# Cross-attention kernel: the products with the value table move ahead of the output pieces in every step

## What is computed

```python
q = heads(x @ W_q);  k_t = heads(text @ W_k);  v_t = heads(text @ W_v)
probs_t  = softmax(einsum('bhsd,bhtd->bhst', q, k_t) * scale)
text_out = einsum('bhst,bhtd->bhsd', probs_t, v_t)
k_ip = heads(ip @ W_k_ip);  v_ip = heads(ip @ W_v_ip)
qsem = l2norm(einsum('bhst,bte->bhse', probs_t, text))
sem  = einsum('bhse,bne->bhsn', qsem, l2norm(ip))
probs_ip = softmax(q_dot_k_ip * scale + 0.5 * sem) * mask
out = (text_out + probs_ip @ v_ip) @ W_out + b_out + x
```

## Time and profile before

| | us |
|---|---|
| median of 3 runs | 1018.13 (1018.01 to 1019.59) |
| the profiled execution | 1019.44 |
| its span | 1017.4 |
| TensorE busy (matmul, weight load) | 967.3, 800.9 |
| VectorE, ScalarE, GpSimd busy | 822.7, 695.2, 659.7 |
| wait of TensorE's U for `pts` | 12.6 in 20 waits |
| wait of VectorE for U | 99.8 in 106 waits |

### The profile page before, as it was taken

The page is one execution under the profiler, slowest core; times in us unless marked ns, Lnnn a source line. Parts: engine busy times, 40 slices in busy tenths (PEclk is TensorE's granted clock), DMA queues, the critical chain, the costliest instruction groups (busy, mean ns, idle before and its releaser), DMA issues.

```text
span 1017.4 us, 24927 instructions
## 1 busy us (share of the span) xinstructions
PE 967.3 (95%) x7684; PEld 800.9 (79%) x7684; DVE 822.7 (81%) x2409; ACT 695.2 (68%) x2332; POOL 659.7 (65%) x1906
## 2 busy tenths in 40 slices
PE   6986888999999999999999999999999999999988
PEld 6865676888888888888878888888878888888855
DVE  5895788888888887888888888878878888888763
ACT  4545787777777777777767777777776777767730
POOL 3342577766766677677766767676766667667761
PEclk9999999999999999999999999999999999999989
DMA  8946999988799989979899989898899988887863
GB/s 283 314 164 140 189 171 197 173 174 173 156 193 192 189 171 184 171 165 176 173 187 175 193 171 177 169 178 170 177 172 191 187 171 188 142 161 137 158 123 111
DMA packets 488147, 180.27 MB, mean 177 GB/s; under 512 B 449694, under 2 KB 467155, under 8 KB 488015
## 3 DMA queue, kind: packets, MB, share of 16 engines
q1 hardware_dynamic: 487983, 178.63, 86.6%
q10 hardware_dynamic: 32, 0.07, 0.0%
HBM read 42.34 MB, written 27.22 MB: 68 GB/s over the span
## 4 chain that ended last, share of the span: by engine, by line
PE 77%; DMA 5%; ACT 3%; DVE 3%; SPq 2%; issue 2%; POOL 0%; DVEq 0%; ACTq 0%
PE ps_Q L1364 25%; PE ps_O L1253 25%; PE ps_S L1274 12%; PE ps_U L1350 11%; DMA pts<-ph 3%; PE ps_M L1290 3%; ACT pr L1034 2%; DMA x_in<-in_x_dram 1%; ACT ph L1046 1%; SPq L947 1%; SPq L910 1%; DVE bias L1156 0%; PE ps_U L1253 0%; SPq L966 0%; DVE x_in L1141 0%
## 5 line engine op out<-in xcount | busy, mean ns | idle before, releaser
L1034 ACT ACTIVATE pr<-ps_S,bias 128x73 f32<-128x73 f32 x1280 | 288.9, 340 | 103.4 <-DVE bias L1156 102.1
L1116 POOL TENSOR_TENSOR ph<-pr,ph 128x220 f16<-128x220 f32 (+1 forms) x640 | 274.1, 460 | 125.8 <-ACT ph L1046 125.8
L1364 PE MATMUL ps_Q<-xT,wq_hi 128*128 128x512 f32 x800 | 279.2, 414 | 6.3 <-DVE qT L1123 6.3
L1253 PE MATMUL ps_O<-wo_hi,aT 128*128 128x320 f16 x1220 | 281.1, 301 | 0.0
L1046 ACT ACTIVATE ph<-pr 128x292 f16<-128x292 f32 x640 | 241.4, 501 | 0.0
L1253 PE MATMUL ps_O<-wo_lo,aT 128*128 128x320 f16 x610 | 183.5, 301 | 0.0
L1364 PEld LDWEIGHTS ps_Q<-xT,wq_hi 128*128 128x128 f32 x800 | 145.6, 190 | 33.4 <-DVE qT L1123 7.6
L1350 PE MATMUL ps_U<-xm,pts 128*128 128x110 f16 (+1 forms) x2560 | 158.8, 212 | 13.3 <-DMA pts<-ph 12.6
L1350 PEld LDWEIGHTS ps_U<-xm,pts 128*128 128x128 f16 (+1 forms) x2560 | 144.4, 98 | 30.5 <-issue 9.2
L1274 PEld LDWEIGHTS ps_S<-kbd,qT 128*128 128x128 f32 x960 | 151.3, 189 | 18.8 <-issue 3.0
L1274 PE MATMUL ps_S<-kbd,qT 128*128 128x308 f32 x960 | 163.7, 305 | 2.6 <-ACT pr L1034 2.1
(11 more groups left out here) (228 smaller groups left out, 1343.2 us busy)
## 6 DMA issues: line engine op xcount, KB each, us to landing
out_dram<-x_in SPq DMA_DIRECT2D x64, 320.0 KB, 2.6
x_in<-in_x_dram SPq DMA_DIRECT2D x56, 320.0 KB, 3.2
pts<-ph SPq DMA_TRANSPOSE x320, 3.4
w_k<-in_L_xattn_W_k_dram SPq DMA_DIRECT2D x5, 512.0 KB, 9.4
w_ip<-in_L_xattn_W_k_ip_dram SPq DMA_DIRECT2D x1, 2560.0 KB, 11.2
w_v<-in_L_xattn_W_v_dram SPq DMA_DIRECT2D x5, 512.0 KB, 8.7
w_ip<-in_L_xattn_W_v_ip_dram SPq DMA_DIRECT2D x1, 2560.0 KB, 10.5
x_in<-in_x_dram SPq DMA_DIRECT2D x2, 1280.0 KB, 5.8
```

Source lines behind the costliest of these rows:

```text
L1034: last = nc.scalar.activation(pr[p % P_RING][:, j, h, :], sc[:, j, h, 0:T], ACT.Exp, bias=bias[p % 2][:, j, h:h + 1], scale=SCALE)
L1116: nc.gpsimd.tensor_tensor(lo, full[:, :, t0:t1], one[:, :, 0, t0:t1], ALU.subtract).then_inc(pl_ready, 1)
L1253: last = nc.tensor.matmul(bank[:, 0:HALF], stationary, moving, start=(k, a, b_) == O_MMS[0], stop=(k, a, b_) == O_MMS[-1])
L1364: last = nc.tensor.matmul(ps_Q[:], wq[a][:, c, k * P:(k + 1) * P], xT[(CC * i + c) % XT_RING][b_][:], start=(c, a, b_) == Q_MMS[0], stop=( ...
```

## The change

In TensorE's loop the block U, with its waits, moves from behind O (and the end pieces) to ahead of O, behind S and M. So the order within a step was S, M, O, U, Q and is S, M, U, O, Q. Nothing else is changed: the same matmuls, semaphores, buffers and the loops of the other engines.

```diff
                     last.then_inc(xT_ready, 1)
 
+                u = pair_of(p - LU)
+                if u is not None:
+
+                    slot = u // 2
+                    k0 = slot % CC
+                    if u % 2 == 0 and slot % SLOTS < CC:
+                        pe.wait_ge(xm_loaded[k0], 32 * (slot // SLOTS + 1))
+                    if u:
+                        pe.wait_ge(attn_ready, u)
+                    else:
+                        pe.wait_ge(xT_lo, CC)
+                    for j in range(2):
+                        pe.wait_ge(*ring(pts_loaded[j], u))
+                        for h in range(HG):
+                            for tile, n in enumerate(STACK):
+                                last = nc.tensor.matmul(uo[:, j, h, :], pts[u % PT_RING][0:n, j, 2 * h + tile, :],
+                                                        xm[0:n, tile, k0 * HG + h, :], start=tile == 0, stop=tile == 1)
+                    last.then_inc(u_ready, 1)
+
                 for i, half, piece in out_at(p):
...
                     if part == 3:
                         last.then_inc(o_ready, 1)
 
-                u = pair_of(p - LU)
-                if u is not None:
...
-                    last.then_inc(u_ready, 1)
-
                 if q_at(p) is not None:
```

## The result

The changed kernel took 1020.17 us in the median (1017.07 to 1025.37), against 1017.98 us (1014.47 to 1021.32) of the kernel before, measured beside it: a ratio of 1.0026 [1.0015, 1.0038]. It is slower by 0.26%, 2.2 us by the medians. Forecast were 1018.9 us and "within 0.2%"; the time lies in the range, 1.3 us above the forecast, and just outside the band of no change. Two kernels further down each had one execution far longer than all its others (1929.69 and 1595.92 us), which their medians leave out.

The account below looks back on a forecast made before the run. The matmul engine's own blocks, one behind the other, were taken as the bound. Terms -8.5 + 1.3 + 6.0 + 2.5 - 0.5 = +0.8 us, applied to the 1018.13 median, gave 1018.9 us; range 1012.0 to 1025.5, the forecast's own 1016 to 1021.

Parts of the forecast that it names:

- joint U to Q becomes O to Q: Steps 16 to 157: O's last matmul covers Q's f32 weight load, saving 0.06 us a step, -8.5 us.
- joint S to U: New joint where U follows the scores: costed at nothing, bound one U matmul, 0.05 us a step.
- waits for VectorE: Middle of the run: the matmul engine doesn't wait for VectorE, so nothing was charged.
- step 16: First step with O: U(14) loses its cover of 12 O matmuls and waits for pts, +1.3 us once.
- three changes of batch: Steps 34-42, 74-82, 114-122: SyncE's queue paces landings, O no longer covers the wait, +2.0 us each, +6.0.
- single late transposes: Nine of 160 pairs, pair 52 standing for them, have pts landing 0.1 to 1.0 us late: +2.5 us.
- end: After S(159): the 2.4 us aT wait goes, about 2 lost as U(158) waits for pts, -0.5 us.
- The sign that I named for it: Profile after, query block: second query matmul comes 0.235 us after the first, not 0.31.
- the upper end: Batch changes at 2.8 us each instead of 2.0: 17 matmuls of cover lost, and half clock after the wait.
- The joints win: Rival: earlier VectorE moves even pairs' landings ahead, late transposes vanish, batch changes cost 1.2 each; 1013.2 us, chance 0.31.
- U waits in every turn: Rival: pts landings late in every turn of ten steps, 0.6 us in each of 14 tiles; 1027.2 us, chance 0.19.
- No joint is gained: Rival: O followed by Q leaves the weight load as open as U did, 0 for -8.5; 1027.4 us, chance 0.12.

Follow-up runs that it names:

- one-matmul order: U placed behind all output matmuls of the step but the last, against the kernel before: 1010.45 us, ratio 0.9922.
- without the loads: Batches 1 to 3 without kbd and xm loads, on batch 0's tables: kernel before 1008.74 us, changed kernel 1004.32, U ahead of the last output matmul 999.43.

## Why the prediction came out as it did, point by point

| term | forecast, us | the runs show |
| --- | --- | --- |
| joint U to Q becomes O to Q | -8.5 | -9.3 (one-matmul order, both without loads) |
| joint S to U | 0 | 0 (0.010 in half of the steps, as S to O had before) |
| waits for VectorE | none | +2.3 (0.12 a turn, and 0.6 in step 151) |
| step 16 | +1.3 | +1.2 (shift of the trace from step 16 to 17) |
| three changes of batch | +6.0 | +6.6 (2.2 each) |
| single late transposes | +2.5 | 1.6 (the view of the waits) to 3.0 (U's distance from S or M) |
| end | -0.5 | +0.3, within 1.3 of nothing |
| sum | +0.8 | +2.2 measured; the rows above give +2.7 to +4.1 |

**The joints.** The mechanism is right. The size, 0.066 us a step instead of 0.06, was within its ends: 0.061 of it is the surplus behind U, worked out below. The sign that I named for it, the distance from the first query matmul to the second, was wrong. I wrote that the second query matmul would come 0.235 us after the first; it comes after 0.34:

```profile
389.45 0.44 PE L1253 MATMUL ps_O<-vw,ipT 128*128 128x320 f16 x2
389.61 0.50 PE L1364 MATMUL ps_Q<-xT,wq_hi 128*128 128x512 f32 x1
389.95 0.40 PE L1364 MATMUL ps_Q<-xT,wq_lo 128*128 128x512 f32 x1
```

The first query matmul is recorded as starting some 30 ns after the start of the one in front of it, whichever that is (two output matmuls 136 ns apart from 389.45, then 389.61), so the distance from the first to the second holds the rest of the one in front. The sum has to be taken over the joint. From the last output matmul to the second query matmul there are 0.367 us, where 0.136 + 0.233 = 0.369 are due: no surplus. Behind U there were 28 + 317 = 345 ns where 51 + 233 = 284 are due: 0.061 us of surplus. That is the number I had from the earlier trace rows, read without the detour.

**S to U at nothing** was right, though by luck. I priced it with a row in which U is followed by O, which is another joint. Behind the last matmul of S the first of U starts 141 ns later, and the second 58 ns after that, 10 more than the 48 behind M or behind O. But S to O had the same 10 ns before the change: an O matmul comes 136 ns after the one in front, and the second one behind S 146 ns after the first.

```profile
336.34 0.31 PE L1253 MATMUL ps_O<-wo_hi,aT 128*128 128x320 f16 x1
336.49 0.30 PE L1253 MATMUL ps_O<-wo_lo,aT 128*128 128x320 f16 x1
```

These two are from the trace before, behind the scores that start at 335.50. So nothing is lost or gained at this joint.

**The waits for VectorE** are the term that I had at nothing without a reason: I wrote that the matmul engine doesn't wait for VectorE here. A plain turn takes 54.93 us with U first and 54.81 in the one-matmul order, and the difference lies in two places. In the steps whose number ends in 7 Q waits for VectorE's part of the query (`qT`, line 1123). Step 137, first after, then in the one-matmul order without the loads:

```profile
856.38 0.68 DVE L1123 TENSOR_TENSOR qT<-ps_Q,qT 128x512 fp32r<-128x512 f32 x1
856.98 0.30 PE L1253 MATMUL ps_O<-wo_hi,aT 128*128 128x320 f16 x1
857.11 0.73 PE L1364 MATMUL ps_Q<-xT,wq_hi 128*128 128x512 f32 x2
...
840.33 0.30 PE L1253 MATMUL ps_O<-wo_hi,aT 128*128 128x320 f16 x1
840.35 0.74 PE L1371 MATMUL ps_Q<-xT,wq_hi 128*128 128x512 f32 x2
```

VectorE is done with `qT` at 857.06, and Q starts 0.13 us behind the last O matmul instead of 0.03. In the steps ending in 9 U starts 0.03 us later behind S than elsewhere, 58 ns after VectorE's `attn`. Together that is the 0.12 us a turn, 1.7 us over 142 steps; in step 151 Q waits another 0.6 us for `qT`. The views of the waits leave the short ones out. What makes VectorE late in the steps ending in 7 is its instruction for the bias (line 1156), just ahead of `qT`: its median there is 1.10 us after the change, 0.31 before and 0.60 in the one-matmul order. Why it takes longer, no run shows. The kernel with U ahead of the last piece has 1.14 us there, and the same wait.

**Changes of batch.** The mechanism (landings paced by SyncE's queue, O no longer beneath the wait) is what the runs show: without the loads the sign of the whole change turns round. Per change 2.2 us against 2.0. The taking back of saved joints is seen best in the one-matmul order, where hardly any cover is lost. From 200 to 950 us it waits 5.2 us for `pts` and 1.3 for `x`, against 3.5 and 1.8 before, and its gain is 7.4 us with the loads where it is 9.3 without: some 1.9 us of the joints is waited away at the three changes, and I had 0.5 us in each. The trace after also shows the half clock that I had left to the upper end, behind a wait of 2 us at step 78:

```profile
518.50:521.90 3.40, 1.30 (x13) 1.09 (x12) 3.23 (x12) 1.89 (x6) 2.70 (x9) 1.00 1.13 252
521.90:525.30 3.40, 3.31 (x24) 2.24 (x22) 2.34 (x8) 3.01 (x12) 2.79 (x11) 0.50 1.10 237
```

The matmul engine was busy 1.30 of 3.40 us at 2.4 GHz, then runs a stretch at 1.2 GHz. Over the runs the mean clock of the kernel after (0.9913) is no lower than that of before (0.9910), so this is no term of the difference here, though up to 1.7 of the 6.5 us read from the two traces; it is one in the kernel with only the batch steps changed.

**Single late transposes.** The sum was right and the places were wrong. Outside step 16 and the batch changes U stands 0.2 to 0.6 us late in seven pairs of the trace after, 3.0 us together (17, 47, 97, 108, 127, 152 and 156). Pair 52, which stood for them in the prediction, shows none. Its step is plain, S, U without a wait, O:

```profile
385.74 1.00 PE L1274 MATMUL ps_S<-kbd,qT 128*128 128x308 f32 x6
386.59 0.98 PE L1309 MATMUL ps_U<-xm,pts 128*128 128x110 f16 x16
387.41 0.30 PE L1253 MATMUL ps_O<-wo_hi,aT 128*128 128x320 f16 x1
```

From issue to landing there are 3.1/3.4/5.2 us after (least, median, most), and 3.1/3.4/5.7 before. Which transpose is late is in part chance and in part not: pair 127 is late in the traces of all five kernels that have U first in the plain steps, pair 97 in three of them, pair 22 in two. The even pairs were helped as supposed: in three of the five positions that even pairs take in a turn, VectorE starts their maximum 0.4 to 0.6 us after the scores instead of 1.1 to 1.2.

**VectorE and the end.** VectorE's wait for U fell from 99.8 to 11.4 us, at no gain, as said. At the end the wait of 2.4 us for `aT` is gone and U waits 2.9 us for `pts` instead (950 to 1017 us), so the end gave nothing, as said.

**The rivals.** "The joints win" had the right joint and missed what VectorE's earlier start does for the changes of batch, which is nothing. "U waits in every turn" did not come for `pts`: 0.7 us of such waits in the 320 us between the batch changes. A wait in every turn did come, but for VectorE and of 0.12 us. "No joint is gained" fell with the kernel that gains 9.3 us by one matmul between U and Q. With it fell my use of a figure of the Trainium skill ("TensorE: Matmul & The Clock Gate", Back-to-back issue gap) as if it held between any two matmuls. That section calls N/2.4 + 2.5 ns the gap of an isolated matmul, and says that in a stream the weight load and the matmul set the spacing together. Inside a block this trace has 51 and 136 ns for its 48 and 136.

**The sum.** It was 1.4 us low: the waits for VectorE took 2.3 us that I had at nothing, the changes of batch 0.6 and the end 0.8 more, and the joint gave 0.8 more; the late transposes lie between 0.9 less and 0.5 more. Most of these are known to about 1 us only. The traces don't add up to the medians exactly either: from the scores of pair 16 to those of pair 157 the trace after is 3.2 us longer than the trace before (791.8 against 788.6). The waits for VectorE are the one term that the rows show to be missing. The forecast's own range, 1016 to 1021, held the time, in part because the joint, sized too small, made up for a fifth of what was missing; that is luck.

**What stays open.** Without the loads the changed order is 4.9 us slower than the one-matmul order, and the traces place it: of 4.6 us between the scores of pairs 16 and 157, 1.8 are in step 16, 1.2 in two late transposes (pairs 127 and 141), 0.6 in Q's wait of step 151 and 0.9 in the short waits for VectorE. That the loads behind the transposes help the one-matmul order is not shown by the times, since the two intervals overlap. The account of the clock rests on the mean over runs, and no kernel was run in which it could be held.

## What to carry to other kernels

A block moved in an in-order queue is worth two accounts: the joints it makes and breaks, and the cover it loses. Here both had one remedy. The joint needs one long matmul behind U, the cover needs the other ten in front, and putting the block ahead of the *last* matmul of its neighbour gives 7.4 us (0.8% by the ratio) where putting it ahead of all of them costs 2.2. An engine with idle time is a third account: here VectorE, idle 16% of the time, still held Q up by 0.1 us in every tenth step once U came first. And microseconds saved on the way to a landing that another queue paces come back only in part: price a saving between such points, not over the whole run. Here 1.9 of 9.3 us were lost that way.

## What the runs showed of the hardware that I had not expected

- Four f32 transposes, each with its own 128x128 f32 weights, follow each other at 109 ns, which I read as the time of the weight load. Behind a matmul of 110 columns (51 ns) Q, whose weights are f32 too, comes 0.061 us late; behind one of 320 columns (136 ns) it does not. That fits a load of 109 ns left open by 58.
- The first query matmul (f32) behind an f16 block is recorded 28 to 30 ns after the start of the one in front; the distance to the second then holds the remainder (0.317 us behind U, 0.338 behind O, for a pitch of 0.233).
- Behind f32 scores, the second matmul of an f16 block comes 10 ns late, whichever block it is: 58 ns instead of 48 for U, 146 instead of 136 for O.
- One VectorE instruction (the bias, 128x8) had a median of 0.31, 0.60 or 1.10 us in the same place of the turn, depending on the order of blocks on TensorE.
- Half-clock stretches of 3.4 us come and go: the order of before had one at each change of batch in one trace (the kernel with only the end changed) and none there in another. Over all the runs, each kernel against its own mean, the time falls by 0.6 to 0.7 us for each 0.001 of mean granted clock; without looking at it, the end of a single profile is read 2 to 3 us wrong.
- One `pts` transpose holds SyncE's queue for 1.23 to 2.76 us, 1.28 in the median, and a table load for some 0.5 (1.98 us for four): two transposes per pair already fill half of a step of 5.5 us. I take this for the reason why the order in this queue gave the changed kernel nothing.
